# Node products over 128 rows, and the tables of layers 1 and 2 waiting for h alone

## The reference

```python
def _nnconv(x, src, dst, edge_attr, ew, eb, rw, rb):
    W = (edge_attr @ ew + eb).reshape(edge_attr.shape[0], x.shape[1], rw.shape[1])
    xj = x[src]
    msg = jnp.einsum('ei,eio->eo', xj, W)
    agg = jax.ops.segment_sum(msg, dst, num_segments=x.shape[0])
    return agg + x @ rw + rb
...
h = relu(layernorm(x))
for i in range(2):
    h = relu(batchnorm(_nnconv(h, ...)))
h = relu(_nnconv(h, ...))
x = x + h @ pred_w + pred_b
h = relu(layernorm(x))
x = x + segment_max(h[src] * edge_weight1, dst) @ W.T + b
```

## Time and profile before

| | us |
|---|---|
| median of three runs | 10234.24 |
| lowest, highest | 10233.40, 10235.42 |
| the profiled execution | 10232.45 |
| its span | 10230.6 |
| mean granted clock in it | 0.961 |

### The profile page before, as it was taken

How to read it: one execution, slowest core, us unless ns; L and a number is a source line. 1 busy time by engine, 2 the same in 40 slices (tenths; PEclk the granted TensorE clock), 3 DMA queues, 4 the chain that set the end, 5 groups by cost and what they waited for, 6 DMA issues and landing times.

```text
span 10230.6 us, 159899 instructions
## 1 busy us (share of the span) xinstructions
PE 9348.9 (91%) x49036; PEld 8493.2 (83%) x49036; DVE 6967.5 (68%) x10638; ACT 6915.7 (68%) x6857; POOL 7502.7 (73%) x7820
## 2 busy tenths in 40 slices
PE   6999999998599999999849999999993999999994
PEld 4888888887388888888738888888883999999994
DVE  7777777777387878787737787878782544444442
ACT  3777777775377777777627777777763887777772
POOL 6777777777577777777747777777775777777776
PEclk9999999999699999999969999999996999999996
DMA  4333333333233333333323333333331211111121
GB/s 114 94 97 97 97 93 97 97 97 81 59 97 98 93 98 96 97 93 97 89 54 93 97 97 97 93 98 96 98 87 22 45 40 40 40 40 40 40 42 20
DMA packets 373818, 808.28 MB, mean 79 GB/s; under 512 B 151096, under 2 KB 211601, under 8 KB 373528
## 3 DMA queue, kind: packets, MB, share of 16 engines
q0 software_dynamic: 250112, 432.57, 20.5%
q1 hardware_dynamic: 123671, 375.30, 11.6%
HBM read 676.39 MB, written 130.92 MB: 79 GB/s over the span
## 4 chain that ended last, share of the span: by engine, by line
PE 50%; issue 17%; POOL 16%; ACT 13%; DVE 2%; DMA 1%; ACTq 0%; POOLq 0%; DVEq 0%; SPq 0%
PE pY L730 41%; POOL gathered L555 16%; PE pY L752 7%; ACT hot_key L615 6%; ACT apart L610 6%; PE pY L472 2%; DMA gathered<-max_table,idx 1%; ACT xeT L801 1%; PE pT L740 0%; ACTq L242 0%; DVE msg L949 0%; PE pT L461 0%; DVE tmp L278 0%; DVE rank L1060 0%; DVE carry_hi L278 0%
## 5 line engine op out<-in xcount | busy, mean ns | idle before, releaser
L730 PEld LDWEIGHTS pY<-part,hot_key 128*128 128x128 f32 x44640 | 8031.1, 188 | 584.2 <-issue 460.2
L730 PE MATMUL pY<-part,hot_key 128*128 128x400 f32 x44640 | 8446.7, 348 | 55.0 <-DVE xe L867 24.2
L555 POOL DMA_INDIRECT gathered<-conv_table,idx x5580 | 5341.8, 957 | 1885.1 <-issue 1593.4
L867 DVE TENSOR_REDUCE xe<-pY 128x16 f32<-128x400 f32 x5580 | 3127.7, 568 | 1416.2 <-PE pY L730 1407.4
L610 ACT ACTIVATE apart<-key_pair,zone_lane 128x1408 f16<-128x1408 f16 (+1 forms) x1984 | 2859.2, 1488 | 1203.2 <-PE pY L730 974.7
L615 ACT ACTIVATE hot_key<-apart,hot_line 128x1408 fp32r<-128x1408 f16 (+1 forms) x1984 | 3048.4, 1584 | 33.2
L555 POOL DMA_INDIRECT gathered<-max_table,idx x1736 | 1670.3, 962 | 601.4 <-issue 536.9
L949 DVE TENSOR_REDUCE msg<-gathered 128x240 f32<-128x2160 f32 x744 | 1558.6, 2095 | 0.2
L278 DVE TENSOR_TENSOR gathered<-pY,pe_attr 128x432 f32<-128x432 f32 x1488 | 775.8, 563 | 633.1 <-PE pY L752 632.8
L801 ACT COPY xeT<-pT 112x128 f32<-112x128 f32 x744 | 188.8, 254 | 1223.5 <-PE pT L740 1223.5
L752 PE MATMUL pY<-edge_w,xeT 48*128 48x432 f32 (+1 forms) x2976 | 736.5, 544 | 143.1 <-ACT xeT L801 143.1
(11 more groups left out here) (133 smaller groups left out, 1621.8 us busy)
## 6 DMA issues: line engine op xcount, KB each, us to landing
key_pair<-key_rows SPq DMA_DIRECT2D x248, 672.0 KB
scanned<-run_pair SPq DMA_DIRECT2D x248, 416.0 KB, 2.5
gathered<-conv_table,idx POOLq DMA_INDIRECT x5580
attr_pair<-in_attr SPq DMA_DIRECT2D x186, 208.0 KB, 2.5
gathered<-max_table,idx POOLq DMA_INDIRECT x1736
key_pair<-key_rows SPq DMA_DIRECT2D x248, 78.0 KB
conv_table<-gathered SPq DMA_DIRECT2D x36, 360.0 KB, 2.3
conv_table<-rows SPq DMA_DIRECT2D x24, 360.0 KB, 2.3
```

Source lines behind the costliest of these rows:

```text
L555: e.indirect_dma_start(out=G[s][:, t, 0:width], out_offset=None, in_=table[:, :], in_offset=bass.IndirectOffsetOnAxis(ap=idx[s][:, t:t + 1 ...
L730: ins = e.matmul(pG[bank], hot_key[s][:, z, at:at + P], part[:, z * NEAR:(z + 1) * NEAR, :], start=(z == 0 and k == 0), stop=(z == ZONES - ...
L867: e.tensor_reduce(xe[s][:, at:at + D], pG[j % BANKS].rearrange("p (r d) -> p d r", d=D), AX.X, ALU.max).then_inc(s_pick.sem, 1)
```

## The change

Two edits.

First, node products become 128 deep. `hs` is 128 columns wide: 80 of h, the constant 1, and 47 columns set to zero once at the start. So the transpose yields 128 rows, ACT copies all of them to `hT`, and `conv_w` and `lin_w` get 47 rows of zeros under their 81 (`diagonal` makes them, and keeps its old depth for `edge_w`). The sums are the same.

Second, `table_product` gets the value of `s_v` from before `parts_of_h` in layers 1 and 2. ACT's first copy of the table then waits for the write to `sink`, not for the third instruction of `parts_of_h`. In layer 0 it waits as before.

```diff
-        conv_w = sb("conv_w", [GB * D + 1, GB * CW])
-        lin_w = sb("lin_w", [GB * D + 1, 2, GB * D])
+        conv_w = sb("conv_w", [P, GB * CW])
+        lin_w = sb("lin_w", [P, 2, GB * D])
...
-        hs = slots(sb, "hs", [P, GB * D + 1])
-        hT = slots(sb, "hT", [GB * D + 1, P])
+        hs = slots(sb, "hs", [P, P])
+        hT = slots(sb, "hT", [P, P])
...
-        INIT_ALL = 2 + 4 * SLOTS
+        INIT_ALL = 2 + 5 * SLOTS
...
-                e.memset(hs[s][:, :], 1.0).then_inc(s_init.sem, 1)
+                e.memset(hs[s][:, 0:GB * D + 1], 1.0).then_inc(s_init.sem, 1)
+                e.memset(hs[s][:, GB * D + 1:P], 0.0).then_inc(s_init.sem, 1)
...
-        def node_product(weights, width, evacuate, wait_weights=None):
+        def node_product(weights, width, evacuate, wait_weights=None, h_ready=None):
...
-            v_ready = s_v.n
+            v_ready = s_v.n if h_ready is None else h_ready
...
-                    e.copy(hT[s][:, :], pT[s][0:GB * D + 1, 0:P]).then_inc(s_hT[s].sem, 1)
+                    e.copy(hT[s][:, :], pT[s][:, 0:P]).then_inc(s_hT[s].sem, 1)
...
-                e.transpose(pT[s][0:GB * D + 1, 0:P], hs[s][:, :], ident[:, :]).then_inc(s_tr[s].sem, 1)
+                e.transpose(pT[s][:, 0:P], hs[s][:, :], ident[:, :]).then_inc(s_tr[s].sem, 1)
...
+            h_ready = s_v.n if layer else None
             v_parts = parts_of_h()
...
-            table_product((s_w, s_w.n) if layer else (s_x, NODE_ALL))
+            table_product((s_w, s_w.n) if layer else (s_x, NODE_ALL), h_ready)
...
-    def diagonal(n, blocks, width, bias):
-
-        out = np.zeros((n * D + 1, n * width), np.float32)
+    def diagonal(n, blocks, width, bias, deep=P):
+
+        out = np.zeros((deep, n * width), np.float32)
...
-        trio = diagonal(TRIO, block[:, :ROW], ROW, bias[:ROW])[:-1]
+        trio = diagonal(TRIO, block[:, :ROW], ROW, bias[:ROW], DEEP + 1)[:-1]
```

More of the change, by code:

```diff
@@ L489, in node_product, with table_product @@
                     bump(c, it)
-        def table_product(wait_weights):
+        def table_product(wait_weights, h_ready):
             def evacuate(pieces, it, b):
@@ L523, in evacuate @@
                 bump(s_tab)
-            node_product(conv_w, CW, evacuate, wait_weights)
+            node_product(conv_w, CW, evacuate, wait_weights, h_ready)
         def residual_product(weights):
```

## The result

| | before | after |
|---|---|---|
| median | 10234.83 us (4 runs) | 10163.88 us (4 runs) |
| lowest, highest | 10233.40, 10237.13 | 10162.30, 10169.08 |
| ratio after to before, 95% interval | | 0.9931 [0.9914, 0.9949] |
| the profiled execution | 10232.45 | 10162.30 |
| its span | 10230.6 | 10160.5 |

The changed kernel is faster by 0.69%, 71 us. The prediction was 10168.5, with a range of 10156 to 10190. In the changed kernel most lines stand one lower: L472 is L471, L461 is L460, L730 is L729. (The last four kernels of the experiments ran on a slower chip, on which the kernel before took 14094 us too, so of those runs only single stages are read.)

What follows compares the result with a forecast made beforehand. TensorE's speed at 1.2 GHz was taken to bound the table stages. Terms -52.2 - 7.6 - 6.0 - 3.0 + 3.1 = -65.7 gave 10166.75 us for the profiled run, 10168.5 us as median; range 10156 to 10190.

Steps and rivals of the forecast that it cites:

- What bounds the kernel now: Table stages, about 58 us each: TensorE's speed at 1.2 GHz is the bound, 57.2 us for 20 groups.
- Depth and clock: Node products: 128 rows instead of 81 raise the clock to 2.4 GHz, as in the carry product, and halve the pace.
- Term 1: Tables of layers 1 and 2: clock rises after 5.0 us, gaining 26.1 us a layer, 52.2 for two.
- Term 2: Tables of layers 1 and 2: start 3.8 us earlier each, 7.6 us for two.
- Term 3: Layer 0: faster table lets the last endpoint compare, waiting for its gather, start earlier; 6.0 us gained.
- Term 4: Edge stages of layers 1 and 2: a warm start gains 2.7 and 0.3 us, together 3.0.
- Term 5: Two residual stages: longer weight loads of transposes cost 0 to 3.1 us, taken as 3.1; no higher clock expected.
- At nothing: Start of the kernel: two memsets, weight loads grown by 162 KB (at most 1.3 us), and hT's copy cost nothing.
- A: Rival: padding doesn't raise the clock, leaving a gain of 4.5 us, 10229.7 us; chance 0.11.
- B: Rival: clock rises but another bound takes over or it drops at times; 17 us less gain, 10185 us; chance 0.09.
- C: Rival: slower than before, the edge loop of TensorE, ACT and POOL settling into a worse phase; about 10255 us; chance 0.02.

Runs made afterwards that it cites:

- experiment 3: The changed kernel with only the node products 128 rows deep, their transposes and copies to hT 81 rows: 10164.31 us, ratio 0.9932.
- experiment 2: The kernel before, 81 rows deep, with only the earlier start of the tables of layers 1 and 2: 10225.36 us, ratio 0.9993.
- experiments 5 to 7: The changed kernel with 96, 97 and 112 rows, in that order, in all node transposes, copies and products: 10163.19, 10167.27 and 10168.10 us.
- 9 and 10: The changed kernel with 82 and 88 rows, in that order, in node transposes, copies and products: 14138.85 and 14303.92 us on the slower chip.
- experiment 12: The changed kernel with six unread 128-deep products ahead of the tables of layers 1 and 2, tables and residuals 81 rows deep: 14258.09 us, slower chip.
- Experiment 1: The changed kernel without the earlier start, so 128-deep products alone: 10168.17 us, ratio 0.9936.
- Experiment 4: The changed kernel with layer 0's table alone back at 81 rows (transpose, copy and product): 10169.15 us, ratio 0.9936.
- experiments 11: The changed kernel with six unread 128-deep products added ahead of the tables of layers 1 and 2: 14198.87 us on the slower chip.

## Why the prediction was right, point by point

**What bounds the kernel now.** Right: TensorE's pace set the tables, 57 us of products in each, and doubling it took 60 us of the two stages.

**Depth and clock.** The argument from the carry product as a twin led to the right forecast; experiment 3 against experiment 2 shows that it is the depth of the product, with all else alike, and experiments 5 to 7, 9 and 10, which change transposes and products together, show where: 82 and 88 rows stay at 0.50, 96, 97, 112 and 128 rise. The reading "an 81-row product can't have the high clock" would have been too wide, and the prediction's wording "what does TensorE need before the clock rises" the right one: experiment 12 shows 81 rows at 2.4 GHz behind deeper work. The rule of the Trainium skill that was weighed there ("TensorE: Matmul & The Clock Gate", Part 1: the clock follows how busy the engine has been) fails in this kernel again, on 57.00 busy us of 57 at 0.50 with 88 rows.

**Term 1**, -26.1 a layer. From the first product to the last, layers 1 and 2 take 31.44 and 31.04 us instead of 57.17: -25.7 and -26.1. Experiment 1, which has the term alone, gives -25.6 and -26.1 by this measure (its -28.04 from sink to gather in layer 2 has 1.9 us of the store's landing in it). The assumed delay of 5.0 us was in the right place: measured 4.5 and 3.7 in the changed kernel, 2.4 to 6.0 over all. By its own row (0.87 in 2741 to 2742) the longest delay that the prediction read was 6.2 us, not 6.1. ("TensorE: Matmul & The Clock Gate", Part 1, in the Trainium skill says that the slow start varies from run to run; here it varies from start to start.) The cover was as thick as read: DVE's copies of successive groups begin 1.455 us apart, against the 1.44 assumed, and DVE waits 0.27 us for products in each group. The one size stated too low is the mean of the 480-column products, 615 and 604 ns instead of 570, which has no term in the sum.

**Term 2**, -3.8 a layer: alone -3.79 and -3.80 from sink to the last product (experiment 2), and -3.95 and -3.85 as the difference of experiment 1 to the changed kernel.

**Term 3**, -6.0: -6.46. The mechanism is the one described: the last compare waits for the last endpoint gather, and starts at 156.28 (156.5 was forecast). Experiment 4 takes it back whole. That the size fits so well is in part luck: the gather lands at 156.26 to 158.86 in the seven kernels, and six of them gained less, down to 3.9 us. TensorE did stop for 14.1 us after its first gather products and started slow again, and the edges of layer 0 lost nothing by it (-0.94 us).

**Term 4**, -2.7 and -0.3: -2.67 and +0.38. The eight kernels behind whose high-clock table layer 1's edges start take 2358.01 to 2358.79 us, the two with a slow table 2361.05 and 2360.03. Layer 2 has 2357.6 to 2358.6 in all ten, slow tables too. That it is TensorE's lead over POOL which does this was argued and not tested. The prediction's 5, for stores of layer 2 that land early, did not come in the changed kernel, where the last one landed late; in experiments 1, 3 and 5 it landed early and the edges took no longer for it (2357.9 to 2358.3 us).

**Term 5**, +3.1, is the step that failed: the residuals took 1.85 and 1.63 us less. Both halves of it were wrong. "Cost 0 to 3.1 us" rested on the transposes' weight loads growing to the mean of the others, with the engine's time growing along. In the slow part of the stage two groups take 1.26 us, 0.63 each against 0.64 before (the distance of DVE's sums): the weight loads of the deep transposes took 183 and 231 ns in turn there, less than the 211 and 258 of before in the same stage, and not 335. That mean was of a line of another product, not a price of depth, and the starting point of 81 columns is itself a dear one: 82 columns take 157 ns in the mean where 81 take 232 (last section). And "I expect no higher clock here" rested on the absence of a row with such a mix; the clock rose half way, behind which two groups take 1.03 us. The term's own alternative, "some 3 us back", was near: 3.48 in the end. What it takes was shown to be narrow: the clock rose in mid-stage only with 128 rows in both transposes and products (experiments 1 and 4 too: 12.5 to 13.4 us), not at 96 to 112 rows and not with thin transposes, where the stages were 13.99 to 14.97.

**At nothing.** The weights grow by 47 rows of 800 and 160 columns, 180 KB and not 162, which changes nothing: the first write to `sink` is at 33.72 us, 33.88 before.

**The sum.** Terms 1 and 2 gave 59.6 (59.8 forecast), term 3 6.5 (6.0), term 4 2.3 (3.0), term 5 3.5 of gain instead of 3.1 of loss, so together 71.8. Against them stands 1.7 us that no term had: 2.67 us more in the edges of the maximum, 0.94 less in those of layer 0. The 2.67 isn't the change's: experiment 2, whose products and edges are code as before, has 2235.35 us there against 2228.96, and the other kernels on the faster chips 2231.3 to 2236.4. The stage scatters by 7.5 us, and the profiled run of before is the lowest seen. The failed term 5 (6.6 us off) was thus covered in part by this scatter, which is luck, and by the range, which had held a residual without its cost (3.1) and with a higher clock (3).

**Rivals.** A fell to experiments 2 and 3: padding does raise the clock, and thin transposes between the products don't prevent it in the tables. B: the group takes 1.455 us, no other bound took over, and once high the clock did not drop within the tables of layers 1 and 2. In layer 0's it did: the record has it high from 92.63 to 96.04 us and again from 102.87 on, which the endpoint gathers hid. C: edges of layers 1 and 2 did not get slower.

**Open.** Where between 88 and 96 rows the step is; why the residuals need more than the tables; the time of the kernel with work ahead of the tables on a faster chip, where the stages point to a gain of 2.0 us in layer 1 and 0.4 in layer 2; and why the last store of layer 2's table lands in 2.25 us in some kernels and in 4.1 to 4.2 in others.

## What to carry to other kernels

Look at the granted clock beside the busy share. If a stage keeps TensorE busy and reads 0.50 all the way, compare the row depth of its products with that of a product that does run at 1.00, and try padding the contraction with zero rows: here going from 81 to 96 rows was enough for the tables and cost nothing there. Where a stage is short, look also at what stands ahead of it: in experiment 12 a clock that was already high was kept by an 81-row table that never raised it. Then ask of each other engine whether it can serve half the pace before counting the gain, and of each stage what is late next, as the endpoint gathers in layer 0, which let through 6.5 us of the 20.9 by which its products got shorter (59.97 to 39.05 us; the prediction had worked out 23).

In reading stages, mind that the timeline merges neighbouring instructions of one kind into a row: the start of such a row is that of its first one.

## What the runs showed of the hardware

An fp32 product of 81 to 88 rows that kept TensorE busy for 57 us didn't raise the clock from 1.2 GHz, one of 96 rows or more did after 2.4 to 6.0 us, and the 81-row one kept a clock that others raised (30 us at 1.00 in layer 1 of experiment 12, 57.0 us at 0.50 in layer 2 of the same run). A pause of 1.43 us behind the table of layer 1 didn't let the clock fall in the changed kernel; pauses of 1.90 and 2.29 us (experiments 11 and 12), each followed by three transposes with 0.60 us of idling between them, did.

The rows cost nothing in the product: 480 columns take 1007 ns at 82 and 88 rows and 1008 at 81, and the table of experiment 12 at 81 rows at the high clock has 571 ns in the mean.

The weight loads of the transposes do depend on their columns, and not in one line. Over the 20 of the first residual, at an unchanged clock of 0.50, they take 157 ns in the mean at 82 columns, 160 at 88, 169 at 96 and 190 at 112, but 232 at 81 and 258 at 97. The stages follow: 13.91, 13.92, 13.99 and 14.17 us against 14.58 and 14.88. At 82 and at 81 columns, both on the slower chip (experiments 9 and 12):

```profile
L460 PEld LDWEIGHTS pT<-ident,hs 128*82 128x82 f32 x20 | 3.1, 157 | 136.4 <-ACT hs L435 135.7
L460 PEld LDWEIGHTS pT<-ident,hs 128*81 128x81 f32 x20 | 4.6, 232 | 136.2 <-ACT hs L435 135.6
```

The two slow counts are the two odd ones, and four even ones rise steadily, so one more zero row, 82 instead of 81, shortens this stage by 0.67 us with no help from the clock. That oddness is the cause rests on two counts and was not tested further.
